# Six softmax sweeps of a graph network: the running sums of a block of nodes stay in one PSUM bank, TensorE adds to them, ScalarE copies them out and scales them by one or zero

## The reference

```python
def gatv2_conv(x, src, dst, Wl, Wr, att, b, heads, c_out):      # layer 0, twice
    xl = (x @ Wl).reshape(n, heads, c_out)
    xr = (x @ Wr).reshape(n, heads, c_out)
    e = leaky_relu(xl[src] + xr[dst], 0.2)
    logit = einsum('ehc,hc->eh', e, att)
    m = segment_max(logit, dst)
    a = exp(logit - m[dst])
    denom = segment_sum(a, dst)
    return segment_sum((a / denom[dst])[:, :, None] * xl[src], dst).reshape(n, -1) + b

# layer 1 (GAT, 8 heads of 32): a = exp(leaky_relu(al[src] + ar[dst]) - max); out = segment_sum(a/sum * xp[src], dst)
# layer 2 (3 times): scores = sum(Q[dst] * (K[src] W_E[type])) / scale * mu; softmax by dst; segment_sum(V[src] * w, dst)
# layer 3 (GIN): agg = segment_sum(x[src], dst), then a dense part; it has no softmax
```

## Time and profile before

| | |
|---|---|
| time, median of 3 runs | 7317.35 us (7316.95 to 7345.25) |
| profiled execution | 7313.39 us |
| its span in the profile | 7311.6 us |
| mean granted clock of TensorE | 0.885 of full speed |

### The profile page before, as it was taken

How to read it: one execution, slowest core, us unless ns; L and a number is a source line. 1 busy time by engine, 2 the same in 40 slices (tenths; PEclk the granted TensorE clock), 3 DMA queues, 4 the chain that set the end, 5 groups by cost and what they waited for, 6 DMA issues and landing times. The chain is left out here.

```text
span 7311.6 us, 115062 instructions
## 1 busy us (share of the span) xinstructions
PE 5467.1 (75%) x25450; PEld 4274.3 (58%) x25451; DVE 4841.4 (66%) x13284; ACT 2775.2 (38%) x9159; POOL 3686.8 (50%) x3856
## 2 busy tenths in 40 slices
PE   2788377769998488856777897777987777867775
PEld 1566366747776266645555685555775555734465
DVE  7666267747776566646999657999559997733313
ACT  0111166635666155523444234443334443300025
POOL 0577277726665177714666105665016663367730
PEclk9999989979999577777999998999999999966677
DMA  1000245546555155635777326776237775023330
GB/s 31 3 3 3 38 151 154 152 81 178 174 172 132 54 159 158 154 79 190 224 225 224 75 70 215 226 226 181 71 99 230 226 227 147 14 84 104 105 56 18
DMA packets 453631, 933.98 MB, mean 128 GB/s; under 512 B 109900, under 2 KB 207110, under 8 KB 453126
## 3 DMA queue, kind: packets, MB, share of 16 engines
q0 software_dynamic: 209536, 582.56, 30.2%
q1 hardware_dynamic: 239520, 346.64, 14.5%
q10 hardware_dynamic: 4326, 2.03, 0.1%
HBM read 789.17 MB, written 141.76 MB: 127 GB/s over the span
## 5 line engine op out<-in xcount | busy, mean ns | idle before, releaser
L1099 PE MATMUL bank<-arena,onehots 128*128 128x264 f32 (+3 forms) x6496 | 2002.7, 439 | 232.3 <-DMA arena<-tab_l,slot_src 120.3
L1055 PE MATMUL bank<-arena,spreads 128*128 x5568 | 1480.8, 375 | 599.9 <-DVE raw L1269 345.5
L1015 POOL DMA_INDIRECT arena<-tab_l,slot_typed x1392 | 1317.3, 946 | 719.7 <-issue 300.8
L1099 PEld LDWEIGHTS bank<-arena,onehots 128*128 128x128 f32 x6496 | 1306.9, 221 | 601.3 <-issue 212.0
L1055 PEld LDWEIGHTS bank<-arena,spreads 128*128 128x128 f32 x5568 | 1030.6, 210 | 980.3 <-issue 857.3
L1015 POOL DMA_INDIRECT arena<-tab_l,slot_src x928 | 884.7, 953 | 478.0 <-issue 259.3
L871 ACT ACTIVATE onehots<-iota_row,slot_loc 128x128 f32<-128x128 f32 x1856 | 641.1, 392 | 948.6 <-PE bank L1099 928.5
L1286 DVE TENSOR_TENSOR acc<-acc,bank 128x264 f32 (+3 forms) x1624 | 654.2, 403 | 504.9 <-PE bank L1099 495.1
L1189 DVE TENSOR_TENSOR arena<-arena,bank 128x512 f32<-128x512 f32 x928 | 630.2, 679 | 181.0 <-ACT stats L1137 75.8
L1015 POOL DMA_INDIRECT arena<-tab_l0b,slot_src x464 | 467.5, 1008 | 349.1 <-POOLq L1503 112.9
L1015 POOL DMA_INDIRECT arena<-tab_l0a,slot_src x464 | 453.8, 978 | 279.3 <-POOLq L1503 122.0
(11 more groups left out here) (376 smaller groups left out, 8078.9 us busy)
## 6 DMA issues: line engine op xcount, KB each, us to landing
spreads<-spread_dram SPq DMA_DIRECT2D x580, 256.0 KB
tab_l<-arena SPq DMA_DIRECT2D x150, 384.0 KB, 3.3
spread_dram<-spreads SPq DMA_DIRECT2D x116, 256.0 KB
onehot_dram<-onehots SPq DMA_DIRECT2D x58, 512.0 KB, 3.7
onehots<-onehot_dram SPq DMA_DIRECT2D x58, 512.0 KB, 4.1
arena<-tab_l,slot_typed POOLq DMA_INDIRECT x1392, 4.1
arena<-tab_l,slot_src POOLq DMA_INDIRECT x928, 2.8
arena<-tab_l0a,slot_src POOLq DMA_INDIRECT x464, 2.6
```

The source lines that it names most:

```text
L1015: pool.indirect_dma_start(out=rows_sb[:, a, t, half:half + width], out_offset=None, in_=table[:, :], in_offset=bass.IndirectOffsetOnAxis(a ...
L1055: mm = pe.matmul(z[x.k % 2][:, t, 0:cw], spreads[:, x.k, t * P:t * P + P], qtab[:, block_no[w], 0:cw], start=True, stop=not gatv2)
L1099: mm = pe.matmul(sums[x.k % 2], onehots[:, x.a, GT * x.k + t, :], rhs, start=t == 0, stop=t == GT - 1)
```

## The change

In the six softmax sweeps (`held = not gin`) there is one running sum, `running = PS[4]`. It is set to zero when a sweep starts. TensorE's matmuls all have `start=False` and add to it. In slot s ScalarE, as the first thing in the slot, waits until group s - 16 is summed, copies `running` to `acc[:, block, :]`, then multiplies `running` in place by `goes_on`, one if the next group belongs to the same block and zero if not (a table worked out once, two more VectorE instructions before the first sweep), and only then signals `added_up`. TensorE waits for `added_up` of the group just before (`needed(x.g)` instead of `needed(x.g - 1)`). VectorE no longer adds; it rescales `running` in the bank before each batch, now in slot 15 of the batch and not 16, and TensorE waits for `rescaled` there.

```diff
+            held = not gin
+            running = PS[4][:, 0:wc]
...
+                            if held:
+                                if needed(x.g):
+                                    pe.wait_ge(S["added_up"].sem, S["added_up"].at(x.g))
+                                if x.k == 0:
+                                    pe.wait_ge(S["rescaled"].sem, S["rescaled"].at(x.batch + 1))
+                            elif needed(x.g - 1):
                                 pe.wait_ge(S["added_up"].sem, S["added_up"].at(x.g - 1))
...
+                                if held:
+                                    mm = pe.matmul(running, onehots[:, x.a, GT * x.k + t, :], rhs, start=False,
+                                                   stop=t == GT - 1, skip_group_check=True)
...
                 def _(act):
...
+                        x = Group(i, w, LAG["keep"])
+                        if x.there and held:
+
+                            act.wait_ge(S["summed"].sem, S["summed"].at(x.g + 1))
+                            op = act.activation(acc[:, block_no[w], 0:wc], running, ACT.Copy)
+                            if not (isinstance(i, int) and x.g == NB * BG - 1):
+                                op = act.activation(running, running, ACT.Copy, scale=goes_on[:, ds(x.g + 1, 1)])
+                            op.then_inc(S["added_up"].sem, 1)
...
-                        x = Group(i, w, LAG["keep"])
-                        if x.there:
+                        x = Group(i, w, LAG["add_up"] if held else LAG["keep"])
+                        if x.there and not (held and x.k > 0):
                             if needed(x.g):
                                 dve.wait_ge(S["added_up"].sem, S["added_up"].at(x.g))
-                            av = acc[:, block_no[x.k if gin else w], 0:wc]
+                            av = running if held else acc[:, block_no[x.k if gin else w], 0:wc]
...
-                                dve.wait_ge(S["rescaled"].sem, S["rescaled"].at(x.batch + 1))
+                                if not held:
+                                    dve.wait_ge(S["rescaled"].sem, S["rescaled"].at(x.batch + 1))
+                        if x.there and not held:
                             dve.wait_ge(S["summed"].sem, S["summed"].at(x.g + 1))
                             dve.tensor_tensor(av, av, sums[x.k % 2], ALU.add).then_inc(S["added_up"].sem, 1)
```

More of the change, by code:

```diff
@@ L101, in gnn_kernel @@
         tile_border = sb("tile_border", [P, NB * 33], BF16)
+        goes_on = sb("goes_on", [P, NB * BG])
         straddle = sb("straddle", [P, NB])
@@ L788, in _ @@
                     link(dve.tensor_scalar(tile_border[:, :], tile_border[:, :], -BIG, None, ALU.mult))
+                    link(dve.memset(goes_on[:, :], 0.0))
+                    link(dve.tensor_tensor(goes_on[:, 1:GRP], block_f[:, 1:GRP], block_f[:, 0:GRP - 1], ALU.is_equal))
                     loc, same = differs[:, 0:NB], differs[:, 32:32 + NB]
@@ L1094, in slot_fn @@
                                 pe.wait_ge(S["denominator_made"].sem, S["denominator_made"].at(x.g + 1))
-                            if needed(x.g - 1):
+                            if held:
[4 more added lines that the diff above has]
+                            elif needed(x.g - 1):
                                 pe.wait_ge(S["added_up"].sem, S["added_up"].at(x.g - 1))
@@ L1098, in slot_fn @@
                                 rhs = rows_sb[:, x.a, GT * x.k + t, 0:wc] if gin else weighted[:, x.k % 2, t, 0:wc]
-                                mm = pe.matmul(sums[x.k % 2], onehots[:, x.a, GT * x.k + t, :], rhs,
-                                               start=t == 0, stop=t == GT - 1)
+                                if held:
+                                    mm = pe.matmul(running, onehots[:, x.a, GT * x.k + t, :], rhs, start=False,
+                                                   stop=t == GT - 1, skip_group_check=True)
+                                else:
+                                    mm = pe.matmul(sums[x.k % 2], onehots[:, x.a, GT * x.k + t, :], rhs,
+                                                   start=t == 0, stop=t == GT - 1)
                             mm.then_inc(S["summed"].sem, 1)
@@ L1106, in _ @@
                 def _(act):
+                    block_no = None
                     def slot_fn(i, w):
+                        nonlocal block_no
+                        if held and w == 0 and not (isinstance(i, int) and G16 * i < LAG["keep"]):
+                            block_no = next_blocks(mybir.EngineType.Activation, 0, G16 * i - LAG["keep"], G16)
+                        x = Group(i, w, LAG["keep"])
[5 more added lines that the diff above has]
+                            op.then_inc(S["added_up"].sem, 1)
                         x = Group(i, w, LAG["turn"])
@@ L1177, in _ @@
                     dve.memset(acc[:, :, :], 0.0).then_inc(step.sem, 1)
+                    if held:
+                        dve.memset(running, 0.0)
                     dve.memset(seg_max[:, :, :], 0.0).then_inc(step.sem, 1)
@@ L1269, in slot_fn @@
                             dve.tensor_reduce(r, lane_split(pr, C), AX, ALU.add).then_inc(S["raw_made"].sem, 1)
-                        if w % (BG if gin else G16) == 0 and not (isinstance(i, int) and G16 * i + w < LAG["keep"]):
+                        if w % (BG if gin else G16) == 0 and not held and not (isinstance(i, int) and G16 * i + w < LAG["keep"]):
                             block_no = next_blocks(mybir.EngineType.DVE, 0, G16 * i + w - LAG["keep"], BG if gin else G16)
-                        x = Group(i, w, LAG["keep"])
-                        if x.there:
+                        x = Group(i, w, LAG["add_up"] if held else LAG["keep"])
+                        if x.there and not (held and x.k > 0):
                             if needed(x.g):
                                 dve.wait_ge(S["added_up"].sem, S["added_up"].at(x.g))
-                            av = acc[:, block_no[x.k if gin else w], 0:wc]
+                            av = running if held else acc[:, block_no[x.k if gin else w], 0:wc]
                             if x.k == 0 and not gin:
```

## The result

The changed kernel takes 7710.16 us (median of 5 runs, 7703.02 to 7761.57), the kernel before 7316.95 us (5 runs, 7307.75 to 7345.25) on the same chip: 1.0544 times as long, interval 1.0503 to 1.0585. So it is slower, as forecast, but by 393 us and not by 258, and 20 us above the top of the range.

A forecast was written before the change was run, and what follows sets the result against it. No engine is always busy and each sweep has another limit, GpSimd in gat, VectorE at 94% in hgt. Terms 170 (gat) + 40 (hgt) + 38 + 10 (gatv2) = +258 us give 7575 us, range 7390 to 7690.

The forecast's parts named there:

- the loss of a batch: hgt: a batch's first sums also wait for VectorE's work up to the rescaling, 2.2 us later; 1.95 us taken.
- its gat part: gat: half-clock loop of 3.19 us with pauses, clock not rising again; mean slot 3.26 us against 2.53, +170 us.
- the term of +40: Three hgt sweeps: loss less gain is net +0.45 us a batch, +40 us; bounds -100 to +60.
- The gain in hgt: hgt: eight additions of 0.34 us a batch leave VectorE, 2.7 us, of which 1.5 us remain because of the loop.
- K: ScalarE: time of the two new instructions, copy 0.29 and scaling 0.46, together 0.75 us; bounds 0.67 to 0.85.
- Second gatv2: Second gatv2 sweep: copy, scaling, hand-over and rescaling lengthen the chain behind each batch's stall; +38 us, bounds +15 to +55.
- First gatv2: First gatv2 sweep: GpSimd hides most of ScalarE's added work; +10 us, bounds 0 to +35.
- The rival of dearer instructions: ScalarE's in-place scaling or unhidden weight loads add 0.3 us in each loop-bound slot; 7715 us, chance 0.08.

The follow-up runs named there:

- experiment 3: Changed kernel without the running sum: two banks, ScalarE copies out and adds nothing, rescaling goes to a spare tile; 7177.24 us, 0.981 times before.
- experiment 9: Changed kernel without ScalarE's scaling by one or zero, `added_up` comes from the copy; 7517.44 us, 1.0273 times before.
- experiment 2: Changed kernel with VectorE's rescaling moved ahead of the slot's weighing, product and reduction, in all sweeps; 7581.97 us, 1.0366 times before.
- experiment 7: Changed kernel with running sums in the hgt sweeps alone and the rescaling moved ahead of VectorE's weighing; 7337.85 us, 1.0024 times before.
- experiment 4: Changed kernel with running sums in hgt alone and three unused 512-column matmuls a batch ahead of the wait for the rescaling; 7402.57 us, 1.0119 times before.
- experiment 1: Changed kernel with one unused 512-column matmul per slot ahead of the wait for the sums, in gat alone; 7555.57 us, 1.0351 times before.
- experiment 6: Changed kernel unedited, run again on the third chip; 7722.9 us, 1.0536 times before.
- experiment 5: On a chip with stand-stills: changed kernel unedited 1.007 times before; hgt-only sums rescaled early 0.9973; that with two fillers a batch 0.9966; changed kernel without scaling 0.9974.

## Why the prediction was wrong in size and right in direction

Cut the hgt sweep at TensorE's sums, from the last matmul of one group to the last of the next. A batch has eight such intervals: the one that ends with its first sums, where the stall for the rescaling is, the two behind it, and five others. The sums over the 29 batches of a sweep, means of the three hgt sweeps, in us (the three parts add up to the sweep within about 2 us):

| kernel | loop | scaling | wait for the rescaling | into the first sums | two behind | clock there | five others | sweep |
|---|---|---|---|---|---|---|---|---|
| before | no | no | no | 49 | 129 | 1.00 | 480 | 656 |
| experiment 3 | no | no | no | 53 | 134 | 1.00 | 428 | 615 |
| experiment 9 | yes | no | yes | 104 | 131 | 0.90 | 443 | 678 |
| experiment 2 | yes | yes | shortened | 81 | 140 | 0.94 | 440 | 661 |
| experiment 7 | yes | yes | shortened | 82 | 140 | 0.94 | 442 | 664 |
| experiment 4 | yes | yes | filled | 122 | 130 | 1.00 | 435 | 687 |
| experiment 1 | yes | yes | yes | 112 | 144 | 0.90 | 443 | 699 |
| after | yes | yes | yes | 114 | 174 | 0.67 | 436 | 725 |

From before to after: +65 into the first sums, +45 in the two intervals behind, -44 in the five others.

- **hgt, the step that failed**, was the loss of a batch: "Something of that was slack; I take 1.95", which is 57 us a sweep. Measured it was 110. The interval with the stall grew by 65 us, 2.2 a batch, so nothing was slack. The two intervals behind it grew by 45 us, 1.6 a batch, with the granted clock at 0.67 where it had been 1.00. For the clock behind the stall the forecast had no term at all, though its gat part rests on just that. The 53 us by which the loss was too small make about 160 of the 166 by which the term of +40 is short of the +206. Its upper bound, +60, left the clock out too. In experiment 1, with the same hgt code at a better clock, the parts are +62, +15 and -37: there too the loss is above 57, and the clock behind the stall is the part that varies.
- **The gain in hgt** was 44 us in the forecast and is 44 in the five other intervals, but that is in part luck. The forecast had eight additions of 0.34 us, of which the loop lets half through. Experiment 3 has no loop and gains only 42 us: the two longest intervals of a batch, with the chain over the maxima, take 8.7 us together before, 8.4 in experiment 3 and 8.4 after. So the relief never was worth 2.7 us a batch. The loop does set a floor, since 1.80 us occurs in experiment 3 and no interval of after is under 2.1 us. Without stall and at full clock, three intervals of 2.14 us a batch and the five others of these kernels (435 to 443) would make about 621 to 629 us. That is an estimate; by it the loop takes back 6 to 14 of the 42 us, and a running sum whose rescaling cost nothing would be faster than before in hgt. No such kernel was run.
- **The scaling in hgt**: after is 47 us a sweep longer than experiment 9, but 43 of them lie in the two intervals behind the stall, at clocks of 0.67 and 0.90. Against experiment 1, with 0.90 in both, it is 20 us.
- **gat** was right in mechanism and, within 19 us, in size. Loop 3.17 us for the 3.19 forecast, K 0.75 as taken (0.29 of the copy, 0.46 of the scaling), hand-over 0.14. The slot with the rescaling is 0.49 us longer (2802.80 to 2806.46), 0.06 a group, for the 0.07 taken. That makes 3.23, and the mean over the 231 intervals is 3.35. The rest is one interval a batch, the sixth, of 4.1 us on average: from the sums at 2795.47 to those at 2799.76 TensorE waits 0.37 us for VectorE's scores (line 1295) and has three more steps of the batch's chain (1074, 1084, 1085), at half clock. Experiment 1 shows the cause and not only the place.
- **Second gatv2**, +51 for +38: the same term, a little under-sized. The scaling makes 27 us of it (740.8 to 713.7 in experiment 9), the one bank and its wait another 27 (713.7 to 686.6 in experiment 3), and without both the sweep is no slower than before. **First gatv2** is +10 as forecast.
- **ScalarE's instructions**: copies of 264 columns took 390 ns (median), of 272 columns 397, and the scaling of 272 columns 459:

```profile
L1131 ACT ACTIVATE acc<-bank x232: 369/390/395, 3665.9 to 4390.3; 128x264 f32 x116
...
L1133 ACT ACTIVATE bank<-bank,goes_on x231: 448/459/462, 2621.0 to 3391.2; 128x272 f32<-128x272 f32 x116
```

  The forecast had 380 and 460. The rival of dearer instructions had a time of 7715, next to the measured 7710, but by a cause that was not there.
- **The clock**: the forecast put the loss of clock into gat alone, and some 14 to 44 us of each hgt sweep are of the same kind (the two intervals behind the stall: 144 us in experiment 1 and 174 in after, 130 in experiment 4 with the stall filled). Where the clock is lost in gat, the idles decide and not the banks, as the forecast read it: with one bank it is 0.50 with the pause and 0.98 with the pause filled (experiment 1). The Trainium skill (TensorE: Matmul & The Clock Gate, A second HAM failure mode) blames cycling through banks with small idles between; here one bank had 0.50 in gat and two banks 0.76 before and 0.73 in experiment 3, so of its two parts the trace bears out the idles.
- **The median** is 51 us under the profiled execution of after. Between executions only the hgt sweeps differ by much (experiments 1 and 6: 693 to 729 us with clocks of 0.93 to 0.86 for the same code), so against the median difference of 393 us the hgt term is about +143, and still over three times the forecast.

What stays open: why the same hgt code is granted 0.93 in one execution and 0.86 in another, and whether the estimate above for a rescaling that costs nothing holds. No version with a running sum was shown to beat before. The early rescaling in hgt alone comes within 0.24% of it (on the chip of experiment 5 it was 0.27% below), and experiment 3, which is 1.9% faster, leaves out the sum.

## What to carry to other kernels

Before moving an accumulation from a side engine into one bank, write down the new loop (produce, hand over, copy, scale, hand back) and put its length beside the shortest slot that the relieved engine would allow: no slot can be shorter than the larger of the two. Do not take the shortest slot for all of them, though: here the relief of VectorE was worth 1.4 us a batch and not 2.7, even without the loop. A loop also takes away the run-ahead that hid short waits, so each stall is then worth its full length plus what TensorE loses while its clock is down, and that second part needs a term of its own. Where TensorE pauses in each slot, look at its granted clock first, since there a filler matmul can be worth more than the instruction that makes it wait.

## What the runs showed of the hardware

- In gat a pause of 0.37 us ahead of the sums in each slot of 3.17 us went with 1.2 GHz for the whole 773 us; one more matmul of 512 columns a slot brought the granted clock to 0.98 and the sweep to 630 us. Where the slot was 0.15 us longer than the 2.67 of unbroken work, and not 0.50, the clock rose sometimes (0.59 on average).
- Single stalls of 2.1 us in hgt were followed by a granted clock of 0.67 in the next two intervals in one execution and 0.90 in another of the same code; it was 0.94 behind stalls of 0.9 us, and 1.00 where fillers took the stall's place.
- A filler has its price: one matmul of 512 fp32 columns took 0.86 us at full clock (2.58 for three), so two of them in a stall of 0.9 us cost what they won back.
- ScalarE's scaling in place in PSUM overlaps the end of the copy: a copy of 397 ns occupies it for 0.29 us before the next starts.
